# Image parts of V and K in pairs of column blocks in a fused cross-attention kernel

## Chip, cores and metric

One core of one Trainium2 chip. The metric is the device time of the program in microseconds (us), given as the median of several runs. The kernel before took 403.87 us (403.3 to 404.85 in 3 runs).

## The reference

Cross attention with 69 text tokens and 8 image tokens (4 dummies, 4 for boxes), 2 batches, 2048 queries, width 640, 20 heads of 32, context width 1024, all in fp32. Text and image tokens have their own projections and their own softmax:

```
q = split_heads(x @ w_q);  k = split_heads(text @ w_k);  v = split_heads(text @ w_v)
out_text = merge_heads(softmax(q k^T / sqrt(32)) v)
k_ip = split_heads(ip_h @ w_k_ip);  v_ip = split_heads(ip_h @ w_v_ip)
out_ip = merge_heads(softmax(q k_ip^T / sqrt(32) + mask_ip) v_ip)
out = (out_text + out_ip) @ w_out + b_out + x
```

The mask comes from which boxes hold a query's place on a 64x32 grid.

## The kernel before

The queries are cut into 8 tiles of 512 (2 batches, 4 tiles each), the width of 640 into 5 column blocks of 128 (4 heads). A unit `c` is one tile and one column block; there are 40. For every unit TensorE (PE) makes q (15 products of 128x512, each operand split in a high and a low part, L637), the scores (L668), O (L682) and the output product (again L637). The work is pipelined: in step `c` PE makes the scores of unit c+1 and q of unit c+2, then O of unit c-2 and, from step 6 on, the output of unit c-6. VectorE (DVE) subtracts the maximum, sums and transposes, ScalarE (ACT) takes the exponential and copies results out of PSUM, GpSimd (POOL) multiplies by the reciprocal sums and makes low parts. SP issues nearly all DMAs; ACT issues four per step. Each engine has one program, written out by hand, with waits on semaphores; the order in each is the order of the code.

K and V are made in the early steps, up to step 5, between the other work: one column block `g` of 128 at a time, five of each. For one block there are

- a text part (`text_part`, L714): eight matmuls, over the context width, 138 columns in a PSUM bank;
- an image part (`image_part`, L720): eight matmuls whose stationary operand is 32 columns of the context (16 image tokens of both batches, padded). Matmul kt writes to the 32 partitions 32*(kt % 4), so that four partial sums stand one below the other in a 128x128 range of a bank, from column 256 (`PART_COL`);
- a copy of this range by ACT to `img_part` (L409 for K, L414 for V);
- a fold (L738, L753): a matmul with a 0/1 matrix that adds the four partial sums into the image columns beside the text part;
- copies, and for V a transposition on PE (L758).

K of block g is made two steps ahead of V of the same block. The blocks of K are in banks 5 and 7, the text and image parts of V in bank 6. The weights come by DMA, 512 KB for each block and kind, into few places: two for K (`wk_raw`, `wki_raw`), three for V (`wv_raw`, `wvi_raw`). A load into a used place waits for a fold that shows the place free: K's block g waits until the fold of block g-2 is done (`kt_made`), V's blocks 3 and 4 for the folds of blocks 0 and 2 (`vt_made`). In SP's program the loads of K's block 4 come in step 0 behind three loads of x.

In steps 0 to 5 (`early_step`) PE has, in this order: the scores; O; the K fold of block c+2; V's text part for c < 3; V's image part of block c-1; four q products; V's fold; five q products; V's transposition; six q products; then for c < 2 K's text and image part of block c+3, otherwise V's text part of block c.

Of the kernel before, what the change touches and what calls it, by code (L numbers as in the profile page):

```python
# [8 lines left out]
ACT = mybir.ActivationFunctionType  # L9
AX_X = mybir.AxisListType.X  # L10

P = 128
# [3 lines left out]
TOKENS = 77  # L16
# [32 lines left out]
def xattn_kernel(nc, x, ctx, bbox, grid, eye, w_q, w_k, w_v, w_k_ip, w_v_ip, w_out, b_out, out):  # L49
# [1 line left out]

    at = {}
    LINE, ROW = 64, W * 4
    top = [-(-nc.sbuf_base // ROW) * ROW]

    def sb(name, shape, dt=F32):

# [13 lines left out]
        return es.enter_context(nc.semaphore(name))  # L71

    with es:
        x_hi = sb("x_hi", [P, BATCH, KD, W], F32R)
        x_lo = sb("x_lo", [P, BATCH, KD, W], F32R)
        o_hi = sb("o_hi", [P, BATCH, KD, W], F32R)
# [13 lines left out]
        eye_sb = sb("eye_sb", [P, P + BATCH * IMG])  # L90
        ident = eye_sb[:, 0:P]
        fold = eye_sb[:, P:P + BATCH * IMG].rearrange("p (b n) -> p b n", b=BATCH)
        vt = sb("vt", [P, BATCH, TOKENS])
        mask = sb("mask", [P, BATCH, TILES, QT, IMG])
        bias = sb("bias", [P, KD])
        box = sb("box", [P, BATCH, BOXES, 4])
# [3 lines left out]
        den = sb("den", [P, 2, 2, QT * HG])  # L100
        rden = sb("rden", [P, 2, 2, QT * HG])
        scratch = sb("scratch", [P, BATCH * TILES * QT * (2 * BOXES + 1) + 2 * BATCH * BOXES])
        img_part = sb("img_part", [P, 2, P])
        res = sb("res", [P, 2, W])


# [15 lines left out]

        WARM_BANK, WARM = 3, 11
        V_BANK, PART_COL = 6, 256
        K_BANKS = [5, 7, 5, 5, 5]
        K_PART_BANKS = [6, 7, 5, 5, 5]
        k_places = [ps[:, bank, 0:BATCH * TOKENS].rearrange("p (b n) -> p b n", b=BATCH) for bank in K_BANKS]
# [242 lines left out]
        @block.scalar  # L370
        def _(act):
            def high(job):

                what, n = job
                number = NUMBER[job]
                slot = stage[:, number % KD, :]
                act.wait_ge(stage_loaded[number % KD], 16 * (number // KD + 1))
                if what == "x":
                    b, _, kt = place(n)
                    if n >= 2 * KD:  # L380
                        act.wait_ge(q_made, (n // KD - 1) * KD)
                    nc.scalar.activation(x_hi[:, b, kt, :], slot[:, 0:W], ACT.Copy).then_inc(stage_hi, 1)  # L382
                else:
                    hi = {"w_q": wq_hi, "w_out": wo_hi}[what]
                    nc.scalar.activation(hi[:, n, :], slot, ACT.Copy).then_inc(stage_hi, 1)

            def copy_q(c):
                act.wait_ge(q_made, c + 1)
                if c >= 2:
                    act.wait_ge(scores_made, c - 1)  # L390
                nc.scalar.activation(q[:, c % 2, :], ps[:, Q_BANK, :], ACT.Copy, scale=SCALE).then_inc(q_copied, 1)  # L391

            def exp(c):
                act.wait_ge(shifted, c + 1)
                nc.scalar.activation(prob[:, c % 2, :, 0:TOKENS], prob[:, c % 2, :, 0:TOKENS], ACT.Exp).then_inc(exp_done, 1)  # L395

            def move_rest(c):

                act.wait_ge(turned, c + 1)
                if c >= 2:  # L400
                    act.wait_ge(o_made, c - 1)
                for a in range(QB):
                    act.dma_start(prob_k[2 * SQ:2 * SQ + SQ // 2, c % 2, a, :, :],  # L403
                                  prob_t[SQ * a:SQ * a + SQ // 2, c % 2, 2, :, :]).then_inc(moved[c % 2], 16)

            def copy_k_part(g):

                act.wait_ge(k_part_made, g + 1)
                nc.scalar.activation(img_part[:, 0, :], ps[:, K_PART_BANKS[g], PART_COL:PART_COL + P], ACT.Copy).then_inc(k_part_copied, 1)  # L409

            def copy_v_part(g):

                act.wait_ge(v_part_made, g + 1)
                nc.scalar.activation(img_part[:, 1, :], ps[:, V_BANK, PART_COL:PART_COL + P], ACT.Copy).then_inc(v_part_copied, 1)  # L414

            def copy_k(g):

                act.wait_ge(kt_made, g + 1)
                nc.scalar.activation(k[:, :, g, :], k_places[g], ACT.Copy).then_inc(k_copied, 1)

            def copy_vt(g):

                act.wait_ge(vt_made, g + 1)
                if g > 0:
                    act.wait_ge(v_made, g)
                nc.scalar.activation(vt[:, :, :], v_place, ACT.Copy).then_inc(vt_copied, 1)

            def copy_v(g):

                act.wait_ge(v_made, g + 1)  # L430
                nc.scalar.activation(v[0:TOKENS, :, P * g:P * g + P], v_turned, ACT.Copy).then_inc(v_copied, 1)

            def o_high(c):
                b, t, g = place(c)
                act.wait_ge(o_made, c + 1)
                if c >= 2 * KD:
                    act.wait_ge(out_made, (c // KD - 1) * KD)
                nc.scalar.activation(o_hi[:, b, g, :], ps[:, O_BANK, :], ACT.Copy).then_inc(o_hi_done, 1)  # L438

            def prologue():  # L440
                high(("w_q", 0))
                for kt in range(KD):
                    act.wait_ge(x0_loaded[kt], 16)
                    nc.scalar.activation(x_hi[:, 0, kt, :], x0_raw[:, kt, :], ACT.Copy).then_inc(x0_hi, 1)
                copy_q(0)
                copy_k_part(0)
                copy_k(0)
                high(("w_q", 1))
                high(("w_q", 2))
                copy_q(1)  # L450
                copy_k_part(1)
                exp(0)
                copy_k(1)
                copy_k_part(2)
                high(("w_q", 3))

            def step(c):
                if c <= KD:
                    if c + AHEAD_K < KD:
                        copy_k(c + AHEAD_K)  # L460
                    if c > 0:
                        copy_v_part(c - 1)
                    if c > 2:
                        o_high(c - 2)
                    if c > 0:
                        copy_vt(c - 1)
                        copy_v(c - 1)
                    exp(c + AHEAD_S)
                    copy_q(c + AHEAD_Q)
                    if c == 2:  # L470
                        o_high(c - 2)
                    if c + AHEAD_K + 1 < KD:
                        copy_k_part(c + AHEAD_K + 1)
                else:
                    o_high(c - 2)
                    if exists(c + AHEAD_S):
                        exp(c + AHEAD_S)
                    if exists(c + AHEAD_Q):
                        copy_q(c + AHEAD_Q)
                if c == 0:  # L480
                    high(("w_q", 4))
                move_rest(c)
                for job in step_jobs(c):
                    high(job)

            def epilogue():
                for c in range(UNITS - 2, UNITS):
                    o_high(c)

            turns(prologue, step, epilogue)  # L490
# [139 lines left out]
        def _(pe):  # L630
# [82 lines left out]
                    text = ctx_sb[:, kt, 0:BATCH * TEXT].rearrange("p (b n) -> p b n", b=BATCH)  # L713
                    nc.tensor.matmul(dst[:, :, 0:TEXT], raw[:, kt, :], text, start=(kt == 0), stop=(kt == KC - 1))  # L714

            def image_part(bank, raw, made):

                for kt in range(KC):
                    rows = slice(IMG_PAD * (kt % 4), IMG_PAD * (kt % 4) + IMG_PAD)
                    last = nc.tensor.matmul(ps[rows, bank, PART_COL:PART_COL + P], ctx_sb[:, kt, BATCH * TEXT:CTX_COLS],  # L720
                                            raw[:, kt, :], start=(kt < 4), stop=(kt >= 4))
                last.then_inc(made, 1)

# [5 lines left out]

            def k_image(g):  # L730
                pe.wait_ge(wki_loaded[g % K_SLOTS], 16 * (g // K_SLOTS + 1))
                image_part(K_PART_BANKS[g], wki_raw[:, g % K_SLOTS, :, :], k_part_made)

            def k_fold(g):
                if g == 0:
                    pe.wait_ge(eye_loaded, 16)
                pe.wait_ge(k_part_copied, g + 1)
                nc.tensor.matmul(k_places[g][:, :, TEXT:TOKENS], img_part[:, 0, :], fold,  # L738
                                 start=True, stop=True).then_inc(kt_made, 1)

            def v_text(g):
# [4 lines left out]

            def v_image(g):
                pe.wait_ge(wvi_loaded[V_SLOT[g]], 16 * (V_ROUND[g] + 1))
                image_part(V_BANK, wvi_raw[:, V_SLOT[g], :, :], v_part_made)

            def v_fold(g):
                pe.wait_ge(v_part_copied, g + 1)
                nc.tensor.matmul(v_place[:, :, TEXT:TOKENS], img_part[:, 1, :], fold, start=True, stop=True).then_inc(vt_made, 1)  # L753

            def v_turn(g):
                pe.wait_ge(vt_copied, g + 1)
# [22 lines left out]
            def early_step(c):  # L779
# [8 lines left out]
                else:  # L788
                    if c < 3:
                        v_text(c - 1)  # L790
                    v_image(c - 1)
                    make_q(c + AHEAD_Q, whole[0:4])
                    v_fold(c - 1)
                    make_q(c + AHEAD_Q, whole[4:9])
# [3 lines left out]
                    make_o(c - 2)  # L798
                if c < 2:
                    k_text(c + AHEAD_K + 1)  # L800
                    k_image(c + AHEAD_K + 1)
                elif c < KD:
                    v_text(c)

# [76 lines left out]
```

## Time and profile before

| | us |
|---|---|
| median of 3 runs | 403.87 |
| profiled execution, whole time | 404.16 |
| its span, first to last instruction | 402.3 |
| PE busy (share of the span) | 393.6 (98%) |
| DVE busy | 336.9 (84%) |
| POOL busy | 156.1 (39%) |
| ACT busy | 129.1 (32%) |
| DMA queue of SP, share of 16 engines | 54.6% |

The chain of work that ended last is PE's for 86%. The mean granted clock of PE is 0.997 of full speed. Matmul durations in the rows overlap each other, since matmuls are pipelined; what one costs is read from start to start. Each fp32 matmul of the image and text parts leaves two records (x16 for eight).

### The profile page before, as it was taken

Reading aid. Unit: us, or ns where it says so; the run is one execution under the profiler, and the core shown is the slowest. Engines: PE = TensorE matmul, PEld = TensorE weight load, DVE = VectorE, ACT = ScalarE, POOL = GpSimd, SP = SyncE. Lnnn points to the kernel's source line nnn. Section 1 sums busy time; section 2 is a strip of 40 time slices with the busy share of each in tenths; the row PEclk is TensorE's granted clock in tenths of the full one; section 3 lists DMA queues with packets and bytes.
Section 4 is the critical chain, followed back from the end, with each engine's and each line's share of the span. In section 5 each row is a group of like instructions: output and inputs, shape, how many; then the busy total and the mean of one; then the engine's idle time right before and its main releaser. Section 6 shows DMA issues by size and latency. Waiting matters only on the chain.

```text
span 402.3 us, 10795 instructions
## 1 busy us (share of the span) xinstructions
PE 393.6 (98%) x4452; PEld 292.3 (73%) x4452; DVE 336.9 (84%) x458; ACT 129.1 (32%) x196; POOL 156.1 (39%) x128
## 2 busy tenths in 40 slices
PE   8899999999999999999999999999999999999995
PEld 7688868577777776777777767777777677776773
DVE  4559779898899998998998999999989999999503
ACT  5236334453333322432323322343223322321100
POOL 0336622687326433364226442462227532222200
PEclk9999999999999999999999999999999999999998
DMA  8999736576657454764457454664466544544555
GB/s 280 382 374 333 206 78 233 158 232 171 182 158 223 132 139 138 196 190 138 137 168 231 124 148 135 209 172 145 121 211 193 142 131 127 156 124 119 178 158 182
DMA packets 42849, 72.96 MB, mean 181 GB/s; under 512 B 10544, under 2 KB 10672, under 8 KB 42800
## 3 DMA queue, kind: packets, MB, share of 16 engines
q1 hardware_dynamic: 37680, 67.02, 54.6%
q10 hardware_dynamic: 5120, 5.25, 5.2%
q8 instruction: 35, 0.57, 0.6%
q14 instruction: 14, 0.11, 0.1%
HBM read 35.53 MB, written 10.49 MB: 114 GB/s over the span
## 4 chain that ended last, share of the span: by engine, by line
PE 86%; DVE 3%; SPq 3%; DMA 3%; ACT 2%; issue 1%; ACTq 1%; DVEq 0%
PE ps L637 63%; PE ps L682 9%; PE ps L668 9%; PE ps L714 3%; SPq L259 2%; DMA wk_raw<-in_w_k 2%; ACT prob L395 1%; PE ps L720 1%; ACTq L403 1%; DVE text_max L501 1%; DVE prob L507 1%; ACT q L391 1%; DMA out_tiles<-res 1%; SPq L279 1%; DMA prob_k<-prob_t 1%
## 5 line engine op out<-in xcount | busy, mean ns | idle before, releaser
L357 POOL TENSOR_TENSOR prob<-prob,rden 128x1104 f32<-128x1104 f32 x40 | 82.2, 2056 | 200.5 <-DVE rden L530 200.5
L395 ACT ACTIVATE prob<-prob 128x1232 f32<-128x1232 f32 x40 | 50.0, 1250 | 65.7 <-DVE prob L518 65.7
L537 DVE STREAM_TRANSPOSE prob_t<-prob 128x1536 f32<-128x1536 f32 x40 | 70.7, 1767 | 0.2 <-POOL prob L359 0.2
L501 DVE TENSOR_REDUCE text_max<-ps 128x16 f32<-128x1104 f32 x40 | 52.1, 1303 | 17.1 <-PE ps L668 16.2
L637 PE MATMUL ps<-x_hi,wq_hi 128*128 128x512 f32 x200 | 59.2, 418 | 0.1
L637 PEld LDWEIGHTS ps<-x_hi,wq_hi 128*128 128x128 f32 x200 | 34.6, 188 | 33.9 <-issue 28.1
L525 DVE TENSOR_REDUCE den<-prob 128x16 f32<-128x1104 f32 x40 | 50.6, 1265 | 7.3 <-ACT prob L395 7.2
L438 ACT ACTIVATE o_hi<-ps 128x512 fp32r<-128x512 f32 x40 | 23.7, 592 | 101.9 <-PE ps L682 98.1
L637 PE MATMUL ps<-o_hi,wo_hi 128*128 128x512 f32 x200 | 55.6, 392 | 0.0
L637 PE MATMUL ps<-o_hi,wo_lo 128*128 128x512 f32 x200 | 55.1, 389 | 0.0
L637 PE MATMUL ps<-o_lo,wo_hi 128*128 128x512 f32 x200 | 55.1, 389 | 0.0
L637 PE MATMUL ps<-x_hi,wq_lo 128*128 128x512 f32 x200 | 54.4, 394 | 0.0
L637 PE MATMUL ps<-x_lo,wq_hi 128*128 128x512 f32 x200 | 52.6, 390 | 0.0
L507 DVE TENSOR_TENSOR prob<-ps,text_max 128x1104 f32<-128x1104 f32 x40 | 52.0, 1300 | 0.0
L341 POOL TENSOR_TENSOR x_lo<-stage,x_hi 128x512 fp32r<-128x512 f32 x35 | 45.1, 1314 | 2.7 <-ACT x_hi L382 2.6
L637 PEld LDWEIGHTS ps<-o_hi,wo_hi 128*128 128x128 f32 x200 | 37.4, 188 | 11.0 <-issue 3.4
L555 DVE SCALAR_TENSOR_TENSOR res<-ps,bias,res 128x512 f32<-128x512 f32 x37 | 27.3, 739 | 19.9 <-DMA res<-in_x 11.7
L682 PE MATMUL ps<-prob_k,v 77*32 77x512 f32 x320 | 43.3, 604 | 0.2
L637 PEld LDWEIGHTS ps<-x_lo,wq_hi 128*128 128x128 f32 x200 | 37.7, 189 | 7.8
L637 PEld LDWEIGHTS ps<-x_hi,wq_lo 128*128 128x128 f32 x200 | 37.6, 189 | 7.9 <-issue 0.2
L637 PEld LDWEIGHTS ps<-o_lo,wo_hi 128*128 128x128 f32 x200 | 37.5, 188 | 7.8
L637 PEld LDWEIGHTS ps<-o_hi,wo_lo 128*128 128x128 f32 x200 | 37.5, 188 | 7.8
(58 smaller groups left out, 346.4 us busy)
## 6 DMA issues: line engine op xcount, KB each, us to landing
prob_k<-prob_t SPq DMA_DIRECT2D x320, 64.0 KB
stage<-in_x SPq DMA_DIRECT2D x38, 256.0 KB, 3.0
res<-in_x SPq DMA_DIRECT2D x37, 256.0 KB
out_tiles<-res SPq DMA_DIRECT2D x37, 256.0 KB, 2.2
prob_k<-prob_t ACTq DMA_DIRECT2D x160, 32.0 KB
wki_raw<-in_w_k_ip SPq DMA_DIRECT2D x5, 512.0 KB, 7.0
wk_raw<-in_w_k SPq DMA_DIRECT2D x5, 512.0 KB, 6.7
wv_raw<-in_w_v SPq DMA_DIRECT2D x5, 512.0 KB, 8.9
```

The costliest lines, as they stand in the source:

```text
L341: nc.gpsimd.tensor_tensor(x_lo[:, b, kt, :], slot[:, 0:W], x_hi[:, b, kt, :].bitcast(F32), ALU.subtract).then_inc(stage_lo, 1)
L357: nc.gpsimd.tensor_tensor(e[:, :, 0:TEXT], e[:, :, 0:TEXT], rden[:, par, 0, :].unsqueeze(2).to_broadcast([P, QT * HG, TEXT]), ALU.mult)
L395: nc.scalar.activation(prob[:, c % 2, :, 0:TOKENS], prob[:, c % 2, :, 0:TOKENS], ACT.Exp).then_inc(exp_done, 1)
L438: nc.scalar.activation(o_hi[:, b, g, :], ps[:, O_BANK, :], ACT.Copy).then_inc(o_hi_done, 1)
L501: nc.vector.tensor_reduce(text_max[:, par, :, :], s[:, :, :, 0:TEXT], AX_X, ALU.max).then_inc(text_max_done, 1)
L507: nc.vector.tensor_tensor(e[:, :, :, 0:TEXT], s[:, :, :, 0:TEXT], text_max[:, par, :, :].unsqueeze(3).to_broadcast([P, QT, HG, TEXT]), ALU ...
L525: nc.vector.tensor_reduce(den[:, par, 0, :], e[:, :, 0:TEXT], AX_X, ALU.add)
L537: nc.vector.transpose(prob_t[:, c % 2, :, :, :].rearrange("p k n r -> p n k r"), prob[:, c % 2, :, :].rearrange("p n (k r) -> p n k r", r= ...
L555: nc.vector.scalar_tensor_tensor(out=tile, in0=ps[:, bank, :], scalar=bias[:, c % KD:c % KD + 1], in1=tile, op0=ALU.add, op1=ALU.add).then ...
L637: return nc.tensor.matmul(ps[:, bank, :], w[:, g, P * kt:P * kt + P], m[:, b, kt, :], start=(n == 0), stop=(n == 3 * KD - 1))
L668: last = nc.tensor.matmul(ps[at:at + P // 2, j, TOKENS * n:TOKENS * n + TOKENS], q[rows, c % 2, P * n + at:P * n + at + P // 2], k[rows, b ...
L682: last = nc.tensor.matmul(ps[DH * j:DH * j + DH, O_BANK, :], v[0:TOKENS, b, P * g + DH * j:P * g + DH * j + DH], p_k[:, :, :, j, :], start ...
```

## The change

It makes the image parts of V's blocks 0 and 1 together in step 1, of blocks 2 and 3 together in step 3, of block 4 alone in step 5; those of K's blocks 3 and 4 together in step 0. K's blocks 0, 1 and 2 stay as they were. The second block of a pair goes to columns 384 to 511 of the same bank. ACT copies both ranges with one instruction of 256 columns, after both are made; `img_part` has room for two per kind. The folds stay one by one, where they were. `img_part` grows by 1 KB per partition; `vt` moves to the front of the memory, before the rounding of x_hi's address to 2 KB. Nothing else is changed, no load either.

```diff
-    top = [-(-nc.sbuf_base // ROW) * ROW]
+    top = [-(-nc.sbuf_base // LINE) * LINE]
...
+        vt = sb("vt", [P, BATCH, TOKENS])
+        top[0] = -(-top[0] // ROW) * ROW
...
-        vt = sb("vt", [P, BATCH, TOKENS])
...
-        img_part = sb("img_part", [P, 2, P])
+        img_part = sb("img_part", [P, 2, 2, P])
...
+        V_PAIRS, K_PAIRS = {0: 2, 2: 2, 4: 1}, {0: 1, 1: 1, 2: 1, 3: 2}
+        V_PLACE, K_PLACE = (0, 1, 0, 1, 0), (0, 0, 0, 0, 1)
...
             def copy_k_part(g):
-                act.wait_ge(k_part_made, g + 1)
-                nc.scalar.activation(img_part[:, 0, :], ps[:, K_PART_BANKS[g], PART_COL:PART_COL + P], ACT.Copy).then_inc(k_part_copied, 1)
+                n = K_PAIRS[g]
+                act.wait_ge(k_part_made, g + n)
+                nc.scalar.activation(img_part[:, 0, 0:n, :], ps[:, K_PART_BANKS[g], PART_COL:PART_COL + n * P].rearrange("p (n d) -> p n d", d=P),
+                                     ACT.Copy).then_inc(k_part_copied, n)
...
-                    if c > 0:
+                    if c - 1 in V_PAIRS:
                         copy_v_part(c - 1)
...
-                    if c + AHEAD_K + 1 < KD:
+                    if c + AHEAD_K + 1 in K_PAIRS:
                         copy_k_part(c + AHEAD_K + 1)
...
-            def image_part(bank, raw, made):
+            def image_part(bank, col, raw, made):
...
-                    last = nc.tensor.matmul(ps[rows, bank, PART_COL:PART_COL + P], ctx_sb[:, kt, BATCH * TEXT:CTX_COLS],
+                    last = nc.tensor.matmul(ps[rows, bank, col:col + P], ctx_sb[:, kt, BATCH * TEXT:CTX_COLS],
...
-                image_part(K_PART_BANKS[g], wki_raw[:, g % K_SLOTS, :, :], k_part_made)
+                image_part(K_PART_BANKS[g], PART_COL + P * K_PLACE[g], wki_raw[:, g % K_SLOTS, :, :], k_part_made)
...
-                nc.tensor.matmul(k_places[g][:, :, TEXT:TOKENS], img_part[:, 0, :], fold,
+                nc.tensor.matmul(k_places[g][:, :, TEXT:TOKENS], img_part[:, 0, K_PLACE[g], :], fold,
...
-                    v_image(c - 1)
+                    for g in range(V_PAIRS.get(c - 1, 0)):
+                        v_image(c - 1 + g)
...
-                    k_image(c + AHEAD_K + 1)
+                    for g in range(K_PAIRS.get(c + AHEAD_K + 1, 0)):
+                        k_image(c + AHEAD_K + 1 + g)
```

`copy_v_part`, `v_image` and `v_fold` change as those of K do.

PE, from the last text part of step 0 (K, block 3) to the scores of step 1 before; `wki_loaded1` and `wki_loaded0` are the semaphores of the two places for K's image weights, block 3 is in the second, block 4 in the first.

```order
L714 MATMUL ps<-ctx_sb,wk_raw 128x2x69 [waits k_copied,wk_loaded1]
L714 MATMUL ps<-ctx_sb,wk_raw 128x2x69 x7
L720 MATMUL ps<-wki_raw,ctx_sb 32x128 [waits wki_loaded1]
L720 MATMUL ps<-wki_raw,ctx_sb 32x128 x7
L668 MATMUL ps<-k,q 64x77 [waits scores_used,k_copied,q_copied]
```

The same place in the changed kernel, up to the scores and the fold behind them.

```order
L721 MATMUL ps<-ctx_sb,wk_raw 128x2x69 [waits k_copied,wk_loaded1]
L721 MATMUL ps<-ctx_sb,wk_raw 128x2x69 x7
L727 MATMUL ps<-wki_raw,ctx_sb 32x128 [waits wki_loaded1]
L727 MATMUL ps<-wki_raw,ctx_sb 32x128 x7
L727 MATMUL ps<-wki_raw,ctx_sb 32x128 [waits wki_loaded0]
L727 MATMUL ps<-wki_raw,ctx_sb 32x128 x7
L675 MATMUL ps<-k,q 64x77 [waits scores_used,k_copied,q_copied]
L675 MATMUL ps<-k,q 64x77 x31
L745 MATMUL ps<-eye_sb,img_part 128x2x8 [waits k_part_copied]
```

The eight image matmuls of block 4 moved up by one step, with their wait for the load, ahead of the scores of step 1.

PE from the end of step 1 (K's text part of block 4) to the q products of step 2, before.

```order
L714 MATMUL ps<-ctx_sb,wk_raw 128x2x69 x7
L720 MATMUL ps<-wki_raw,ctx_sb 32x128 [waits wki_loaded0]
L720 MATMUL ps<-wki_raw,ctx_sb 32x128 x7
L668 MATMUL ps<-k,q 64x77 [waits scores_used,k_copied,q_copied]
L668 MATMUL ps<-k,q 64x77 x31
L738 MATMUL ps<-eye_sb,img_part 128x2x8 [waits k_part_copied]
L714 MATMUL ps<-ctx_sb,wv_raw 128x2x69 [waits v_copied,wv_loaded1]
L714 MATMUL ps<-ctx_sb,wv_raw 128x2x69 x7
L720 MATMUL ps<-wvi_raw,ctx_sb 32x128 [waits wvi_loaded1]
L720 MATMUL ps<-wvi_raw,ctx_sb 32x128 x7
L637 MATMUL ps<-x_hi,wq_hi 128x512 [waits stage_lo,q_copied]
```

The same place in the changed kernel.

```order
L721 MATMUL ps<-ctx_sb,wk_raw 128x2x69 x7
L675 MATMUL ps<-k,q 64x77 [waits scores_used,k_copied,q_copied]
L675 MATMUL ps<-k,q 64x77 x31
L745 MATMUL ps<-eye_sb,img_part 128x2x8 [waits k_part_copied]
L721 MATMUL ps<-ctx_sb,wv_raw 128x2x69 [waits v_copied,wv_loaded1]
L721 MATMUL ps<-ctx_sb,wv_raw 128x2x69 x7
L644 MATMUL ps<-x_hi,wq_hi 128x512 [waits stage_lo,q_copied]
```

Both groups of image matmuls are gone from here; V's went one step up, K's to the place shown before.

ACT from the copy of q in step 0 to the copy of V's first image part, in the changed kernel.

```order
L394 ACTIVATE q<-ps 128x512 [waits scores_made,q_made]
L413 ACTIVATE img_part<-ps 128x256 [waits k_part_made]
L388 ACTIVATE wq_hi<-stage 128x640 [waits stage_loaded4]
L406 DMA prob_k<-prob_t 16x512 [waits turned]
L406 DMA prob_k<-prob_t 16x512 x3
L385 ACTIVATE x_hi<-stage 128x512 [waits stage_loaded0]
L385 ACTIVATE x_hi<-stage 128x512 [waits stage_loaded1]
L385 ACTIVATE x_hi<-stage 128x512 [waits stage_loaded2]
L426 ACTIVATE k<-ps 128x2x77 [waits kt_made]
L420 ACTIVATE img_part<-ps 128x256 [waits v_part_made]
```

The order is that of before; the two copies into `img_part` had 128 columns, and the first of them now waits for both blocks of K.

## Rows read from the trace of the kernel before

**Rows 1.** Windows view, 26 to 32 us: busy time (instructions) by engine, clock, DMA, GB/s

```profile
26.00:32.00 6.00, 6.00 (x49) 5.07 (x48) 5.93 (x7) 1.85 (x3) 3.95 (x3) 1.00 0.97 356
```

**Rows 2.** Chain that ended last: start us, us, what; one steady step's products

```profile
80.49 7.04 PE ps L637 x30
```

**Rows 3.** Timeline of PE: start us, us, what [idle before <-releaser]; the two late gaps

```profile
74.60 0.40 PE L753 MATMUL ps<-eye_sb,img_part 128*128 128x16 f32 x2 [0.17 <-ACT img_part L414]
...
78.54 0.95 PE L668 MATMUL ps<-k,q 32*64 32x77 f32 x64 [0.71 <-ACT q L391]
```

**Rows 4.** Timeline of PE, end of step 0

```profile
29.55 2.04 PE L714 MATMUL ps<-ctx_sb,wk_raw 128*128 128x138 f32 x16
31.52 0.65 PE L720 MATMUL ps<-wki_raw,ctx_sb 128*32 128x128 f32 x16
32.23 0.95 PE L668 MATMUL ps<-k,q 32*64 32x77 f32 x64
```

**Rows 5.** Timeline of SP, the issues of K's block 4

```profile
26.87 0.45 SPq L246 DMA_DIRECT2D wk_raw<-in_w_k  x1
27.36 0.74 SPq L246 DMA_DIRECT2D wki_raw<-in_w_k_ip  x1
```

**Rows 6.** DMA view, 27.2 to 27.8 us: issue, count, size, us to landing

```profile
wki_raw<-in_w_k_ip SPq DMA_DIRECT2D x1, 512.0 KB, 7.8
```

**Rows 7.** Chain that ended last, first text weights of K

```profile
4.49 7.85 DMA wk_raw<-in_w_k
12.38 2.15 PE ps L714 x16
```

**Rows 8.** Timeline of PE, steps 1 to 6, what stands around the image parts

```profile
42.21 0.64 PE L720 MATMUL ps<-wki_raw,ctx_sb 128*32 128x128 f32 x16
42.78 0.95 PE L668 MATMUL ps<-k,q 32*64 32x77 f32 x64
...
43.91 2.13 PE L714 MATMUL ps<-ctx_sb,wv_raw 128*128 128x138 f32 x16
45.97 0.65 PE L720 MATMUL ps<-wvi_raw,ctx_sb 128*32 128x128 f32 x16
46.54 1.20 PE L637 MATMUL ps<-x_hi,wq_hi 128*128 128x512 f32 x4
...
60.67 2.04 PE L714 MATMUL ps<-ctx_sb,wv_raw 128*128 128x138 f32 x16
62.64 0.95 PE L668 MATMUL ps<-k,q 32*64 32x77 f32 x64
63.52 1.06 PE L682 MATMUL ps<-prob_k,v 77*32 77x512 f32 x8
64.40 0.62 PE L720 MATMUL ps<-wvi_raw,ctx_sb 128*32 128x128 f32 x16
64.95 1.20 PE L637 MATMUL ps<-x_hi,wq_hi 128*128 128x512 f32 x4
...
79.42 1.06 PE L682 MATMUL ps<-prob_k,v 77*32 77x512 f32 x8
80.42 1.42 PE L637 MATMUL ps<-x_hi,wq_hi 128*128 128x512 f32 x5
```

**Rows 9.** Timeline of ACT, the copy of K's image part of block 3

```profile
32.24 0.28 ACT L409 ACTIVATE img_part<-ps 128x128 f32<-128x128 f32 x1
```

**Rows 10.** Timeline of PE, start of the span

```profile
1.05 5.06 PE L764 MATMUL ps<-q 128*128 128x128 f32 x22 [1.05 <-DVE q L592]
...
6.65 0.63 PE L637 MATMUL ps<-x_hi,wq_lo 128*128 128x512 f32 x1
7.08 0.43 PE L637 MATMUL ps<-x_lo,wq_hi 128*128 128x512 f32 x1
```

**Rows 11.** Windows view, end of the span (columns as rows 1)

```profile
397.00:398.00 1.00, 0.47 (x3) 0.04 (x1) 1.00 (x2) 0.00 (x0) 0.00 (x0) 1.00 0.01 2
...
400.00:401.00 1.00, 0.00 (x0) 0.00 (x0) 0.00 (x0) 0.00 (x0) 0.00 (x0) 0.50 1.04 399
```

More of the change, by code:

```diff
@@ L406, in copy_k_part @@
             def copy_k_part(g):
-                act.wait_ge(k_part_made, g + 1)
-                nc.scalar.activation(img_part[:, 0, :], ps[:, K_PART_BANKS[g], PART_COL:PART_COL + P], ACT.Copy).then_inc(k_part_copied, 1)
+                n = K_PAIRS[g]
+                act.wait_ge(k_part_made, g + n)
+                nc.scalar.activation(img_part[:, 0, 0:n, :], ps[:, K_PART_BANKS[g], PART_COL:PART_COL + n * P].rearrange("p (n d) -> p n d", d=P),
+                                     ACT.Copy).then_inc(k_part_copied, n)
             def copy_v_part(g):
-                act.wait_ge(v_part_made, g + 1)
-                nc.scalar.activation(img_part[:, 1, :], ps[:, V_BANK, PART_COL:PART_COL + P], ACT.Copy).then_inc(v_part_copied, 1)
+                n = V_PAIRS[g]
+                act.wait_ge(v_part_made, g + n)
+                nc.scalar.activation(img_part[:, 1, 0:n, :], ps[:, V_BANK, PART_COL:PART_COL + n * P].rearrange("p (n d) -> p n d", d=P),
+                                     ACT.Copy).then_inc(v_part_copied, n)
             def copy_k(g):
@@ L748, in v_image @@
                 pe.wait_ge(wvi_loaded[V_SLOT[g]], 16 * (V_ROUND[g] + 1))
-                image_part(V_BANK, wvi_raw[:, V_SLOT[g], :, :], v_part_made)
+                image_part(V_BANK, PART_COL + P * V_PLACE[g], wvi_raw[:, V_SLOT[g], :, :], v_part_made)
             def v_fold(g):
                 pe.wait_ge(v_part_copied, g + 1)
-                nc.tensor.matmul(v_place[:, :, TEXT:TOKENS], img_part[:, 1, :], fold, start=True, stop=True).then_inc(vt_made, 1)
+                nc.tensor.matmul(v_place[:, :, TEXT:TOKENS], img_part[:, 1, V_PLACE[g], :], fold, start=True, stop=True).then_inc(vt_made, 1)
             def v_turn(g):
```

## The prediction

> **What bounds the kernel now.** I read the busy shares first. TensorE (PE) works 98% of the span, and the loads are heavy early: from 26 to 32 us PE is busy for all 6.00 us while the DMA engines are 97% taken at 356 GB/s [rows 1]. In the chain of work that ended last the steady part reads as one pattern repeated: scores, O, thirty 128x512 products in 7.04 us, 0.235 us each [rows 2]. In the timeline of PE hardly a gap is left: after the first 16 us there are two, 0.17 us at 74.6 and 0.71 us before the scores at 78.54 [rows 3]. The second is short of a reserve: it ends when ScalarE has copied q, and q's copy stands behind the exponential and the copy of V, which PE's own transposes released shortly before, so it moves along with PE. So the kernel is bound by PE's order, from the first step to the end. A microsecond in which PE must wait in the early steps is a microsecond at the end, and a microsecond of PE work taken out is one gained. VectorE and ScalarE have slack in these steps and follow PE.
>
> What has to be looked at is therefore (a) how long the image matmuls hold PE, alone and behind each other, and (b) whether their weights are there at the earlier places.
>
> **The K pair: the weights of block 4 are not there.** Before, PE begins step 0's last text part at 29.55, block 3's eight image matmuls at 31.52 and the scores at 32.23 [rows 4]. Block 4's image matmuls came a whole step later, at 42.21 [rows 8]. Now they stand between the image matmuls of block 3 and these scores. Their load is issued by SP at 27.36 [rows 5], since it waits for the third K fold and stands behind three loads of x and the text weights; the change moves no row of SP. Its time to landing was 7.8 us [rows 6]. These 7.8 us count from the start of the issue: the first text weights of K, issued at 4.49, land after 7.85 us, at 12.34, and PE begins on them at 12.38, 0.04 later [rows 7]. So block 4's image weights land at 27.36 + 7.8 = 35.16 and PE can start on them at 35.20. Eight such matmuls up to the start of the scores take 42.78 - 42.21 = 0.57 us [rows 8]. The scores start at 35.77 in place of 32.23: **+3.54 us**.
>
> What of this is hidden? Nothing on PE: the wait stands at the head of its queue, and behind it are the scores of unit 2, the K fold, V's text part and all the rest. On ScalarE the copy of the K parts, which ran at 32.24 [rows 9], now asks for both blocks and waits until about 35.8. Queued behind it are the rounding of the last block of w_q, four DMAs of step 0's probabilities, three roundings of x, a copy of K and the first copy of V parts. They slide by about 3.6 us, as PE's own places for them do (the q product that needs w_q's last block comes a step later), so I charge nothing more. VectorE gets its scores 3.5 us later; it was itself behind with unit 1 when they came, so it loses less than that and stays ahead of PE's demand. SP's load of V's block 3, whose guard is V's first fold, slips with PE; it is used two steps later.
>
> The landing itself could move. Down: the four DMAs of ScalarE, 32 KB each, no longer start at 32.24 but after the wait, and their 0.13 MB at 356 GB/s [rows 1] are 0.37 us of the engines. Up: nothing new is ahead of the load. So the delay lies between 3.17 and 3.54 us by this; I take 3.54, since the engines serve other queues as well and the share that falls to this load is not shown. On this the Trainium skill says, in Trainium Kernel Development and Optimization, Key Constraints, that DMAs issued from SP, ACT and POOL run on the same 16 engines and interleave. By that rule the load would land up to 0.37 us earlier and the time would be lower by as much; the trace of before doesn't show this load without those four.
>
> **What comes back at the later places.**
> - K, step 1: block 4's image matmuls are gone. Text part to scores with nothing between is 62.64 - 60.67 = 1.97 us [rows 8]; text part to image matmuls is also 31.52 - 29.55 = 1.97 [rows 4]. What goes is 42.78 - 42.21 = 0.57: **-0.57**. (Their work at the new place is inside the 3.54.)
> - V, step 2: block 1's go. Before: 45.97 - 43.91 = 2.06 and 46.54 - 45.97 = 0.57 [rows 8], together 2.63 from the text part to the q products; without them I take 1.97, the longer of what a text part costs here: -0.66.
> - V, step 4: block 3's go. Before, O to image is 64.40 - 63.52 = 0.88 and image to q 64.95 - 64.40 = 0.55; O to q directly is 80.42 - 79.42 = 1.00 [rows 8]: -0.43.
> - Added at steps 1 and 3: a second eight directly behind the first. A row of sixteen isn't in the trace. From below, eight matmuls that need no change of the array's form cost 0.88 + 0.55 - 1.00 = 0.43, the net figure just seen; from above 0.57, the price when alone. I take 0.43, because both boundaries of a pair are already paid for by the first eight: +0.86.
> - Sum for V: -0.66 - 0.43 + 0.86 = **-0.23** (from above +0.05).
> - ScalarE loses three copies and has three of 256 columns for 128, hidden: in V's places four q products of over 1 us stand between the image matmuls and the fold.
> - vt moves ahead of x_hi in memory: an address, no instruction; nothing.
>
> Without any effect on the clock: 3.54 - 0.57 - 0.23 = **+2.74 us**.
>
> **The clock.** The stall makes PE idle from about 32.15 (31.52, 0.43 and the last matmul's tail) to 35.20, some 3.05 us, longer than any gap of before. What does that do? At the end of the span PE's last matmul ends at about 397.5 and the granted clock is 0.50 over all of 400 to 401 [rows 11]: it fell from 2.4 to 1.2 GHz at most 2.5 us after PE went idle. So a pause of 3.05 us is long enough for it to fall. The price from below is 0 (it doesn't fall, or rises as soon as PE works). From above: at the start PE works from 1.05 on, and products still start 0.43 us apart at 6.65 and 7.08 [rows 10], against 0.235 later [rows 2]; some 6.0 us at half pace give away (1 - 0.235/0.43) x 6.0 = 2.7 us. The pause is a single one in a busy stretch, nearer to neither end; I take the middle, **+1.4 us**. The Trainium skill, TensorE: Matmul & The Clock Gate, The HAM clock gate, says likewise that the array runs at 1.2 GHz after it was idle and gets back to 2.4 GHz after sustained activity. By that rule the fall is to be expected and the sum stays as it is; that a single pause in the middle of the work does it, no row of this kernel shows.
>
> **Sum.** 404.16 (the profiled execution's own time; its span is 402.3, with 1.9 around it) + 2.74 + 1.4 = 408.3. The profiled execution is 0.29 over the median of the runs shown (403.87). Against that median: **408.0 us**, 1% slower.
>
> **Rivals.**
> 1. *The pause costs only itself.* The clock stays at 2.4 GHz, as it did through the 0.71 us gap of rows 3. For it: the pause is short, and the fall at the end came with nothing at all behind it. Against: the 2.5 us of rows 11. Time: 403.87 + 2.74 = 406.6. With the load 0.37 us earlier 406.2.
> 2. *The clock stays low for as long as at the start.* 403.87 + 2.74 + 2.7 = 409.3, and a little more if the pair's second eight cost 0.57 each (409.6).
> 3. *Not slower: the transfer is there.* The mechanism: block 4's image weights land before PE comes to them, because the load, issued at 27.36, gets a larger share of the engines in this program. The place is the end of step 0 and the price is that of the whole stall: without it K gives 0.43 - 0.57 = -0.14, V -0.23, and the time is 403.5. It decides from a landing 3.2 us earlier on (by 31.95, in 4.6 us rather than 7.8); with one only 0.72 us earlier and no loss by the clock the result comes within 0.5% of before. Against it: the row before shows all engines at 97% in this stretch, the same loads stand ahead of it in the same order, and nothing is removed from them before 32.2.
> 4. *The lost time is caught up later.* The early steps hold waits of PE of 0.88 us in all, and those come from ScalarE's place behind PE. If both vanished, 405.7 with no clock effect. I give it little.
>
> **Chances.** Forecast (stall with a fall of the clock that costs 0.7 to 2.2): 0.50, 407.3 to 408.9. Rival 1: 0.27. Rival 2: 0.13. Rival 3: 0.04. Rival 4: 0.06. A measurement of this kernel tells about 0.5% (2.0 us) from no change. Slower than that, above 405.9: all of the forecast, of rival 2 and nearly all of rival 1, 0.89. Within: part of 1, 3 and 4, 0.10. Faster, under 401.9, has no mechanism beyond 0.37 us: 0.01. The range: 406.0 (rival 1 with an early landing) to 409.9 (rival 2 with a dearer pair) leaves out rivals 3 and 4 and some at the top.
>
> **What would show it.** In the profile after: PE's row of sixteen image matmuls of K broken by a wait of about 3.1 us for the DMA into wki_raw, the scores behind it at about 35.8 (anything before 33 and the main term is wrong); the waits table with that DMA as PE's largest single one; the granted clock at half for a stretch between 34 and 41 us, with products 0.43 us apart (at 1.00 throughout, rival 1); text to scores in step 1 at 1.97 with nothing between; V's pairs 1.0 us long rather than 1.14; the steady step still 8.9 to 9.0 us. The prediction is wrong if the load's landing isn't at 35, if the lag of 2.74 at 43 us isn't the lag at 300 us, or if steps 1 to 5 run shorter than PE's rows say.

## The result and the profile after

The changed kernel took 409.34 us in the median (407.76 to 410.76, 6 runs), the kernel before 403.94 us (402.83 to 404.85, 6 runs). The ratio is 1.0133 (95% interval 1.0102 to 1.0164). Forecast were 408.0 us and a range of 406.0 to 409.9. The profiled execution took 409.87 us, its span is 408.1 (before 404.16 and 402.3), so it is one of the longer ones.

The page gives the granted clock of PE in tenths of full speed, for 40 equal slices of the span, here of 10.2 us each. In the kernel before only the last slice is under 9; after, the fourth (30.6 to 40.8 us) is at 7.

```profile
span 408.1 us, 10795 instructions
...
PEclk9997999999999999999999999999999999999999
```

The timeline of PE, in the stretch of [rows 4] and on through [rows 8] (start us, us, what, idle before and what ended it):

```profile
30.82 2.15 PE L721 MATMUL ps<-ctx_sb,wk_raw 128*128 128x138 f32 x16 [0.95 <-DMA wk_raw<-in_w_k]
32.90 0.65 PE L727 MATMUL ps<-wki_raw,ctx_sb 128*32 128x128 f32 x16
36.38 1.08 PE L727 MATMUL ps<-wki_raw,ctx_sb 128*32 128x128 f32 x16 [2.83 <-DMA wki_raw<-in_w_k_ip]
37.38 1.42 PE L675 MATMUL ps<-k,q 32*64 32x77 f32 x64
...
39.18 3.90 PE L721 MATMUL ps<-ctx_sb,wv_raw 128*128 128x138 f32 x16
43.01 1.08 PE L727 MATMUL ps<-wvi_raw,ctx_sb 128*32 128x128 f32 x32
44.02 1.21 PE L644 MATMUL ps<-x_hi,wq_hi 128*128 128x512 f32 x4
...
48.02 2.04 PE L721 MATMUL ps<-ctx_sb,wk_raw 128*128 128x138 f32 x16
49.99 0.95 PE L675 MATMUL ps<-k,q 32*64 32x77 f32 x64
...
51.12 2.13 PE L721 MATMUL ps<-ctx_sb,wv_raw 128*128 128x138 f32 x16
52.99 1.17 PE L644 MATMUL ps<-x_hi,wq_hi 128*128 128x512 f32 x4
```

The scores, at 32.23 in [rows 4], start at 37.38. Between the two image groups of K stands the wait for `wki_raw`, and what follows is slow: V's text part takes 43.01 - 39.18 = 3.83 us, where it took 2.06 in [rows 8]. From 44.02 on the durations are the old ones. The windows view of the same stretch (us, then busy time and instructions of PE, PEld, DVE, ACT, POOL, then the granted clock, DMA share and GB/s) says why:

```profile
34.00:35.00 1.00, 0.00 (x0) 0.00 (x0) 0.04 (x1) 0.00 (x0) 0.88 (x1) 1.00 1.00 401
35.00:36.00 1.00, 0.00 (x0) 0.00 (x0) 0.00 (x0) 0.00 (x0) 1.00 (x1) 0.99 1.05 410
36.00:38.00 2.00, 1.62 (x53) 1.21 (x56) 0.00 (x0) 0.42 (x2) 0.55 (x2) 0.50 1.07 299
...
42.00:43.00 1.00, 1.00 (x6) 0.87 (x4) 1.00 (x2) 0.06 (x1) 1.00 (x2) 0.60 0.57 154
43.00:44.00 1.00, 1.00 (x33) 0.81 (x32) 1.00 (x1) 0.00 (x0) 1.00 (x2) 1.00 0.23 72
```

The clock fell just before 36, in the wait, and rose in the last quarter of 42 to 43: some 6.8 us at 0.50, that is at 1.2 GHz, nearly all of it under work. The load itself, in the timeline of SP and in the DMA view of the issues at 28.4 to 28.6 us, as [rows 5] and [rows 6]:

```profile
28.46 0.89 SPq L249 DMA_DIRECT2D wki_raw<-in_w_k_ip  x1
```

```profile
wki_raw<-in_w_k_ip SPq DMA_DIRECT2D x1, 512.0 KB, 7.9
```

It was issued 1.1 us later than in the profile of before and took as long, 28.46 + 7.9 = 36.4. The change touches no load; the text weights of block 3 were late too (the 0.95 us in the first row above). In the profiles of the kernels below whose loads are in the same order this issue stands anywhere from 27.43 to 29.03 us, and the load lands 6.3 to 8.0 us behind it, so this is how much one execution differs from another. A late issue need not be a late landing: with the latest, at 29.03, PE began on the weights at 35.33.

Most of the lag stays. The same scores, before and after:

```profile
301.77 0.95 PE L668 MATMUL ps<-k,q 32*64 32x77 f32 x64
```

```profile
307.54 0.95 PE L675 MATMUL ps<-k,q 32*64 32x77 f32 x64
```

They are 5.77 us apart, and the two profiled times differ by 409.87 - 404.16 = 5.71.

### The profile page after: what moved, and what is told of

Read it like the earlier page. It is cut to its first block, busy times and chain, and to the rows that moved or that the text cites. A ratio compares the mean times of both kernels' runs of the same rounds, so it can differ in the third digit from the quotient of the medians.

```text
span 408.1 us, 10795 instructions
## 1 busy us (share of the span) xinstructions
PE 394.8 (97%) x4452; PEld 294.4 (72%) x4452; DVE 337.4 (83%) x458; ACT 128.9 (32%) x193; POOL 155.7 (38%) x128
## 4 chain that ended last, share of the span: by engine, by line
PE 82%; DMA 7%; SPq 5%; DVE 3%; issue 1%; ACT 1%; ACTq 1%; DVEq 0%
PE ps L644 59%; PE ps L675 9%; PE ps L689 8%; PE ps L721 4%; SPq L262 2%; DMA out_tiles<-res 2%; DMA wk_raw<-in_w_k 2%; DMA wki_raw<-in_w_k_ip 2%; PE ps L727 1%; DVE prob_t L544 1%; DMA res<-in_x 1%; ACTq L406 1%; DVE text_max L508 1%; DVE prob L514 1%; SPq L249 1%
## 5 line engine op out<-in xcount | busy, mean ns | idle before, releaser
L562 DVE SCALAR_TENSOR_TENSOR res<-ps,bias,res 128x512 f32<-128x512 f32 x37 | 27.2, 736 | 19.5 <-DMA res<-in_x 11.4
```

Source lines behind the costliest of these rows:

```text
L562: nc.vector.scalar_tensor_tensor(out=tile, in0=ps[:, bank, :], scalar=bias[:, c % KD:c % KD + 1], in1=tile, op0=ALU.add, op1=ALU.add).then ...
```

## The experiments

Theory A was the prediction's: all of the loss arises at K's pair, from PE's wait for block 4's image weights and from the clock that falls in it. Against it stood: pairs cost by themselves (B), V's block 1 comes too early (C), the clock is of no matter, ScalarE's queue behind its longer wait has a share. Ratios are to the kernel before in the same comparison, with 95% intervals.

### The pairs of V alone

```diff
-        V_PAIRS, K_PAIRS = {0: 2, 2: 2, 4: 1}, {0: 1, 1: 1, 2: 1, 3: 2}
-        V_PLACE, K_PLACE = (0, 1, 0, 1, 0), (0, 0, 0, 0, 1)
+        V_PAIRS, K_PAIRS = {0: 2, 2: 2, 4: 1}, {g: 1 for g in range(KD)}
+        V_PLACE, K_PLACE = (0, 1, 0, 1, 0), (0, 0, 0, 0, 0)
```

> The pairs of V alone; the image parts of K one by one at their old places. Theory A (the time is lost at K's pair: the wait for the image weights of block 4 and the clock that falls behind it): no wait for wki_raw and no fall of the clock before the end of the span; 403.7 us, between 403.2 and 404.2 (V's rows give 0.23 us less than before). Theory B (sixteen image matmuls in a row, or one copy for two blocks, cost by themselves): two of the three pairs are still there, so most of the loss stays, 407 us or more. Theory C (a part of the loss is V's block 1 made before its place): 1 to 2 us over before.

Measured: 403.47 us, ratio 0.999 (0.9965 to 1.0014). B and C fall. PE's timeline:

```profile
35.89 1.08 PE L727 MATMUL ps<-wvi_raw,ctx_sb 128*32 128x128 f32 x32
36.90 1.20 PE L644 MATMUL ps<-x_hi,wq_hi 128*128 128x512 f32 x4
...
44.59 2.13 PE L721 MATMUL ps<-ctx_sb,wv_raw 128*128 128x138 f32 x16
46.46 1.18 PE L644 MATMUL ps<-x_hi,wq_hi 128*128 128x512 f32 x4
```

A pair takes 36.90 - 35.89 = 1.01 us, against 0.57 for one block: the second eight cost 0.44, the estimate's 0.43. With nothing between, V's text part to q takes 1.87 us, where 1.97 was taken. V's two pairs therefore save 0.3 us, which is too little for this measurement to show.

### The pair of K alone

```diff
-        V_PAIRS, K_PAIRS = {0: 2, 2: 2, 4: 1}, {0: 1, 1: 1, 2: 1, 3: 2}
-        V_PLACE, K_PLACE = (0, 1, 0, 1, 0), (0, 0, 0, 0, 1)
+        V_PAIRS, K_PAIRS = {g: 1 for g in range(KD)}, {0: 1, 1: 1, 2: 1, 3: 2}
+        V_PLACE, K_PLACE = (0, 0, 0, 0, 0), (0, 0, 0, 0, 1)
```

> The pair of K alone; V's image parts one by one. Theory A: PE waits about 3 us for wki_raw before block 4's image matmuls, the granted clock falls to half for a stretch behind it, and all of the loss is there and 0.2 us more: 409.5 us, between 407 and 411. Theory B: one pair of three, about a third of the loss, 405.7 us.

Measured: 409.17 us, ratio 1.0133 (1.0104 to 1.0161), the ratio of the whole change. PE's timeline:

```profile
31.83 0.65 PE L727 MATMUL ps<-wki_raw,ctx_sb 128*32 128x128 f32 x16
35.33 1.08 PE L727 MATMUL ps<-wki_raw,ctx_sb 128*32 128x128 f32 x16 [2.85 <-DMA wki_raw<-in_w_k_ip]
...
42.49 1.19 PE L644 MATMUL ps<-x_hi,wq_hi 128*128 128x512 f32 x4
```

From the end of the wait to the q products of step 1 it takes 42.49 - 35.33 = 7.16 us. At the full clock this is 0.57 for the eight [rows 8] and 35.98 - 32.23 = 3.75 from the scores [rows 4] to these products in the kernel before, 4.32 together. The clock costs the difference, 2.84 us. The products in the kernel before, and the text part that follows them:

```profile
35.98 1.20 PE L637 MATMUL ps<-x_hi,wq_hi 128*128 128x512 f32 x4
...
40.24 2.04 PE L714 MATMUL ps<-ctx_sb,wk_raw 128*128 128x138 f32 x16
```

### The wait filled with useless work

```diff
                     for g in range(K_PAIRS.get(c + AHEAD_K + 1, 0)):
+                        if g == 1:
+                            for _ in range(12):
+                                nc.tensor.matmul(ps[:, V_BANK, :], wq_hi[:, 0, 0:P], x_hi[:, 0, 0, :], start=True, stop=True)
                         k_image(c + AHEAD_K + 1 + g)
```

> The whole change with twelve extra products of 128x512 into the idle bank 6 between the image matmuls of block 3 and those of block 4 (some 2.8 us of work that is of no use; nobody reads it). The wait for the load becomes short, its end stays where it was. Theory A with the clock's share: the scores of step 1 start as late as in the changed kernel, but the clock stays at full speed, and the time is 406.6 us (405.8 to 407.3), about 2 to 3 under the changed kernel. Rival (the clock doesn't matter, or the loss is all the wait): the same time as the changed kernel, 409.3 us. If the work is added behind the wait rather than inside it, 412 us.

Measured: 406.22 us, ratio 1.0059 (1.0023 to 1.0095). More work on PE, and the kernel is some 3 us faster than the changed one. PE's timeline:

```profile
32.66 3.02 PE L812 MATMUL ps<-x_hi,wq_hi 128*128 128x512 f32 x12
35.94 0.64 PE L727 MATMUL ps<-wki_raw,ctx_sb 128*32 128x128 f32 x16 [0.26 <-DMA wki_raw<-in_w_k_ip]
36.51 0.95 PE L675 MATMUL ps<-k,q 32*64 32x77 f32 x64
...
40.70 1.19 PE L644 MATMUL ps<-x_hi,wq_hi 128*128 128x512 f32 x4
```

The load arrives no earlier than in the run of K's pair alone (35.94 and 35.33). But the eight image matmuls take 0.57 and the q products start 40.70 - 35.94 = 4.76 us after them, which is 0.57 + 3.75 and the 0.44 of V's second eight: nothing is slow. Its windows have the granted clock at 1.00 from 32 to 44 us. This separates the two parts of the loss: the wait alone, with the small savings of the pairs in it, is worth 406.22 - 404.17 = 2.05 us, the clock the remaining 3 or so. The filling doesn't hold the clock up for certain: one of the six runs took 408.31 us, with a mean granted clock of 0.994 where the other five have 0.999 or 1.000. It has no trace, so where its clock fell is not known.

### The kernel before with the wait alone, bare and filled

```diff
             def early_step(c):
+                if c == 1:
+                    pe.wait_ge(wki_loaded[0], 48)
                 make_scores(c + AHEAD_S)
```

> The kernel before with one thing more: PE waits, ahead of the scores of step 1, until the image weights of K's block 4 have landed. No image matmul is moved, no pair is made, ScalarE waits for nothing new. Theory A: this wait and the clock behind it are the whole loss of the pair of K; PE stands still for about 3 us, the clock falls to half, and the time is 409 us (407 to 410.5). Rival (what is queued on ScalarE behind the copy for both blocks has a share in the loss): clearly less, 406 to 407.

Measured: 408.19 us, ratio 1.011 (1.0062 to 1.0158). This kernel has no pair, and ScalarE waits for nothing new, and it has most of the loss. Its four runs are far apart, 406.34 to 410.73. PE's timeline:

```profile
35.06 1.25 PE L668 MATMUL ps<-k,q 32*64 32x77 f32 x64 [2.98 <-DMA wki_raw<-in_w_k_ip]
...
40.37 1.20 PE L637 MATMUL ps<-x_hi,wq_hi 128*128 128x512 f32 x4
```

Here 5.31 us pass from the scores to the q products instead of 3.75: 1.56 for the clock, about half of what the pair of K paid. The windows view shows it back at full speed from just before 39 us on, after some 3.4 us:

```profile
35.00:36.00 1.00, 0.94 (x64) 0.94 (x64) 0.00 (x0) 1.00 (x3) 1.00 (x2) 0.72 0.99 385
36.00:38.00 2.00, 2.00 (x26) 1.84 (x14) 1.66 (x3) 0.86 (x3) 2.00 (x3) 0.50 1.08 321
38.00:39.00 1.00, 1.00 (x7) 1.00 (x7) 1.00 (x1) 0.00 (x0) 1.00 (x2) 0.58 1.02 262
39.00:40.00 1.00, 1.00 (x16) 0.86 (x18) 0.93 (x3) 0.00 (x0) 1.00 (x2) 1.00 1.13 215
```

With the twelve products of the run above placed before this wait as well:

```diff
                 if c == 1:
+                    for _ in range(12):
+                        nc.tensor.matmul(ps[:, V_BANK, :], wq_hi[:, 0, 0:P], x_hi[:, 0, 0, :], start=True, stop=True)
                     pe.wait_ge(wki_loaded[0], 48)
```

> As the kernel before with the wait alone, and twelve useless products of 128x512 in front of it, into the idle bank 6. Theory A: PE is busy through the time of the wait, the clock stays, and what is left is the late start of the scores: 406.5 us (405.7 to 407.3), 2 to 3 under the kernel with the bare wait. Rival (the clock is no matter): both alike.

Measured: 406.18 us, ratio 1.006 (1.0039 to 1.0082), the same as the changed kernel filled. The two kernels with the wait bare and the two with it filled agree within their intervals, although one of each has the pairs and the other hasn't. So ScalarE's queue has no share that these runs can show.

The four runs of the bare wait also show that the clock need not fall. A stretch of 3.4 us at half speed takes 3.4 x 0.5 / 405 = 0.004 off the mean of an execution. The quickest run, 406.34 us, has a mean of 0.998, too high for such a stretch, and the time of the filled kernels; the slowest, 410.73 us, has 0.991.

### The load at another time

If the late load is the cause, an earlier load must cure it with all pairs in place. First with a place of its own, in `o_hi`, issued before the loads of x:

```diff
+        wki4_raw = over("wki4_raw", "o_hi", [P, KC, P])
...
                 load_k(3, wki_raw, w_k_ip, wki_loaded)
+                sp.dma_start(wki4_raw[:, :, :], w_k_ip[KD - 1]).then_inc(wki4_loaded, 16)
...
-                    load_k(4, wki_raw, w_k_ip, wki_loaded)
...
             def k_image(g):
+                if g == KD - 1:
+                    pe.wait_ge(wki4_loaded, 16)
+                    image_part(K_PART_BANKS[g], PART_COL + P * K_PLACE[g], wki4_raw[:, :, :], k_part_made)
+                    return
```

> The whole change, but K's image weights of block 4 get a place of their own (in o_hi, which is empty until step 2) and their load is issued in the prologue, before the three loads of x, with no wait for a fold. Theory A: they are issued near 25.4 and land near 32.5, so PE waits 0 to 1 us, the clock stays at full speed, and the time is 403.5 to 404.7 us, most likely 404.0. Theory B: pairs as before, so 408 to 410 us.

Measured: 403.44 us, just under the expected range, ratio 0.9984 (0.9967 to 1.0). The timelines of SP and of PE:

```profile
25.15 0.44 SPq L305 DMA_DIRECT2D wki_raw<-in_w_k_ip  x1
```

```profile
31.37 0.65 PE L729 MATMUL ps<-wki_raw,ctx_sb 128*32 128x128 f32 x16
32.47 0.65 PE L729 MATMUL ps<-wki_raw,ctx_sb 128*32 128x128 f32 x16 [0.46 <-DMA wki_raw<-in_w_k_ip]
33.04 0.95 PE L677 MATMUL ps<-k,q 32*64 32x77 f32 x64
```

A wait of 0.46 us remains. To remove it, the load goes still further up, behind V's block 1 in the prologue:

```diff
                 load_v(1, wvi_raw, w_v_ip, wvi_loaded)
+                sp.dma_start(wki4_raw[:, :, :], w_k_ip[KD - 1]).then_inc(wki4_loaded, 16)
```

> The whole change with a place of its own for K's image weights of block 4, as in the run before, but their load is issued still earlier, behind V's block 1, near 18.6 us. Theory A: they have long landed at 32 and PE waits for nothing there; the wait of 0.46 us of the run before is gone: 403.0 us, if the other loads are not later for it. Against it: the 512 KB ahead of the text weights of block 3 make these land about 1.3 us later, and PE waits for them before step 0's last text part: 404.3 us.

Measured: 405.1 us, 0.8 over the expectation's dearer side, ratio 1.0019 (0.9996 to 1.0041). In the profile the wait is gone, and another stands in its place, for the text weights one part earlier.

```profile
31.18 2.15 PE L723 MATMUL ps<-ctx_sb,wk_raw 128*128 128x138 f32 x16 [0.88 <-DMA wk_raw<-in_w_k]
33.25 1.08 PE L729 MATMUL ps<-wki_raw,ctx_sb 128*32 128x128 f32 x32
34.26 0.95 PE L677 MATMUL ps<-k,q 32*64 32x77 f32 x64
```

That is what the second side of the expectation named. One profile doesn't show it to be the cause, since the changed kernel, with these weights' load at its old position, waited 0.95 us for them too.

Last, the old places and the old guard, and only the order of SP's loads in step 0 changed:

```diff
+                if c == 0:
+                    load_k(4, wki_raw, w_k_ip, wki_loaded)
                 for job in step_jobs(c):
                     load(job)
                 if c == 0:
                     load_k(4, wk_raw, w_k, wk_loaded)
-                    load_k(4, wki_raw, w_k_ip, wki_loaded)
```

> The whole change, the old places, but SP issues the image weights of block 4 first in step 0, ahead of the three loads of x and of the text weights of block 4. Theory A: the load goes out when the third K fold is done, at 26.2 to 26.5 instead of 27.4 to 28.5, and has 1.25 MB less ahead of it; it lands at 32.5 to 34, PE waits 0.5 to 2 us, the clock stays in most runs: 404.5 us (403.5 to 405.5). Rival (the guard on the place, not the order of the loads, makes it late): 407 or more.

Measured: 403.41 us, just under the expected range, ratio 0.9988 (0.997 to 1.0006). The wait is 0.48 us:

```profile
31.55 0.64 PE L728 MATMUL ps<-wki_raw,ctx_sb 128*32 128x128 f32 x16
32.68 0.65 PE L728 MATMUL ps<-wki_raw,ctx_sb 128*32 128x128 f32 x16 [0.48 <-DMA wki_raw<-in_w_k_ip]
33.25 0.95 PE L676 MATMUL ps<-k,q 32*64 32x77 f32 x64
```

So the guard on the place is not what made it late; its position behind three loads of x and one of text weights is. None of these loads was needed soon: behind the 0.48 us PE waits for no DMA up to 90 us.

### Is a version better than both?

The two good versions once more, with 12 runs each and 23 of the kernel before.

> The kernel with the loads reordered once more, in more rounds, to see whether it is under the kernel before and not only level with it. From PE's rows: its pairs save 0.23 (V) and 0.14 (K), its wait for the load costs 0.5, so 0.1 us either way: a ratio to before of 0.9985 to 1.001. A gain by over 0.2% would mean that something else than the image parts is better in it.

> The kernel with a place of its own for block 4 once more, in more rounds. The same sum, with a wait of 0.46 us: a ratio to before of 0.9985 to 1.001.

Measured: reordered 403.34 us, ratio 0.9979 (0.9963 to 0.9994); own place 403.48 us, ratio 0.9982 (0.9965 to 0.9999). Both are just under the expected range, and under the kernel before by some 0.2%, 0.7 us, with intervals that just exclude no change. The sum from PE's rows gave 0.1; with the 1.87 us measured for V's text part it is V 0.31 + K 0.13 - the wait. That wait varies: it was 0.46 and 0.48 us in the profiles above, 0.37 in the new one of the reordered kernel and none in that of the own place, so the sum is 0 to 0.4 us. Whether the rest comes from the pairs or from the other order of the loads is open: the kernel before with its loads alone reordered was not tried.

## Why the prediction was right

The time lies in the range and the mechanism is the one forecast, at its place. The number is not the forecast's: 409.34 lies above its 407.3 to 408.9 and where rival 2 stood (409.3, chance 0.13). That it still lies in the range is in part luck, since errors cancel in the sum below. Step by step, for the profiled execution:

- *The bound.* A delay of PE in step 1 is one at the end: the lag is 6.0 us at 80 us, 5.77 at 300 and 5.71 in the profiled times.
- *The landing and the start of the scores.* Forecast: PE on block 4 at 35.20, scores at 35.77. Measured: 36.38 and 37.38; in K's pair alone 35.33. The time to landing was right in this profile (7.9 for 7.8) and is not a constant (6.3 in K's pair alone, issued at 29.03), the time of issue was that of one execution, and the eight matmuls ran at half clock (1.00 for 0.57). The possible gain of 0.37 us by ScalarE's postponed DMAs did not show: the load took 7.9, 6.3 and 8.0 us where they came behind it (changed kernel, K's pair, filled) and 7.8 and 7.6 where they were issued from 32.2 us on (kernel before, bare wait). The Trainium skill (Trainium Kernel Development and Optimization, Key Constraints) has the DMAs of SP, ACT and POOL interleave on the same 16 engines; no run here shows what that is worth.
- *What comes back.* K: text part to scores 49.99 - 48.02 = 1.97, as forecast. V: the second eight 0.44 for 0.43; the text part in front of q 1.87 for 1.97, 0.1 us too dear. V in all: -0.31 for -0.23.
- *The wait without the clock.* +2.74 was forecast for it; the filled kernel has 2.05 (0.9 to 3.8 by the interval of its ratio). The forecast is within it. The wait filled in the kernel before has 406.18 - 403.94 = 2.24. One thing that it could not see: in the profile of before the first O, in step 2, took 1.71 us, in every other profile here 1.06 or 1.07, so about 0.64 us of the path of that one execution are not paid elsewhere. What made it slow there stays open. The row of before:

```profile
50.62 1.71 PE L682 MATMUL ps<-prob_k,v 77*32 77x512 f32 x8
```

- *The clock.* This is the term that was mis-sized: "I take the middle, +1.4 us", between 0 and 2.7. Measured are 2.84 in K's pair alone and 1.56 in the kernel with the bare wait; for the changed kernel, from 36.38 to the q products at 44.02 are 7.64 us, where 0.57 + 3.75 + 0.44 = 4.76 are due at the full clock, so 2.88. It came out at the upper bound, rival 2's 2.7, in the profiled executions of both kernels with the pair, and near the middle in the one without. The mean granted clock of the six runs of the changed kernel was 0.990 to 0.994, against 0.996 or more in all but one run of the kernel before, so it fell in each of them, and by different lengths. Both grounds of this step were weaker than it took them to be. The 2.7 us rest on products 0.43 us apart at the start of the span; the windows view of before has the granted clock at 1.00 from 0 to 10 us, so half speed is read from the spacing alone, and that 2.7 is nearly 2.88 may be chance. The row of before for the place of these products:

```profile
6.00:7.00 1.00, 1.00 (x3) 0.83 (x3) 0.12 (x1) 0.77 (x2) 0.00 (x0) 1.00 0.99 367
```

And that 3.05 us are "long enough for it to fall" rests on the end of one span. After the last matmul of the changed kernel the clock still stood at 1.00 for over 4 us:

```profile
403.47 0.39 PE L644 MATMUL ps<-o_lo,wo_hi 128*128 128x512 f32 x1
```

```profile
407.00:408.00 1.00, 0.00 (x0) 0.00 (x0) 0.00 (x0) 0.00 (x0) 0.00 (x0) 1.00 0.04 12
```

So a pause of 3 us can bring the fall and need not; rival 1's chance was a real one.

- *The sum.* Forecast +4.1 on the median of before, measured +5.4 (409.34 - 403.94): the clock's 2.88 for 1.4 is about the difference, but other errors cancel beside it. From the profile of before to that of after the lag of PE is 4.15 us at block 4's image matmuls (36.38 - 32.23), and 8.04 at the q products of step 1 (44.02 - 35.98); in between come 0.57 and 0.44 for the second eights of K and V and the clock's 2.88. Then 0.57 of K go, as forecast, and 0.76 of V in step 2, for 0.66. So do the 0.64 us of the slow O, and 0.26 between the first q products of step 1 and K's text part (40.24 - 35.98 = 4.26 before, 48.02 - 44.02 = 4.00 after). V's second pair adds 0.43 and step 4 gives it back, which leaves 5.81. Against the forecast the landing is 1.2 us and the clock 1.5 us too long, and 0.9 us came back that no step of it had. The landing varies: in K's pair alone PE began at 35.33.

Rival 1 (the clock stays) is what the filled kernels show, at 406.2 instead of 406.6, but not the changed kernel. Rival 3 (the transfer is there) is what the load experiments made: 403.4, where it said 403.5. Rival 4 (caught up later) is wrong in its mechanism: the two waits of [rows 3] are still there, with 0.24 and 0.69 us. But the lag does shrink at other places, by the 0.26 and 0.64 us above, in steps 1 and 2.

## What to carry to other kernels

An operation that is pulled forward takes its wait for data along: before an edit that saves tenths on the engine, compare the landing of each load with the new place, and where it is late look for loads ahead of it in its queue that can wait. Here one load moved ahead of four others was worth 6 us, and the pairs some tenths at most. And a pause of about 3 us on TensorE cost up to twice its length here, because the work behind it ran at half clock; where it could not be removed, work that does nothing was better than none.

## What the runs showed of the hardware

- One pause of TensorE of 2.8 to 3.0 us in an otherwise full stretch brought the granted clock from 2.4 to 1.2 GHz, in all three profiled executions that had one. By the mean granted clock it did so in the six runs of the changed kernel, but not in one of the four with the bare wait (0.998, 406.34 us). Pauses of up to 1.21 us did not, in any profile.
- The length of a pause alone does not decide it. After the last matmul of a span the clock fell 2.2 us later in the kernel before, 2.5 to 3.9 in seven others and 4.2 in the changed kernel; in the other three (own place, both filled ones) it had not fallen when the span ended, 3.6 to 4.3 us after that matmul.
- The low stretch that follows differs in length: some 6.8 us in two of the three (cost 2.84 and 2.88 us of PE time), some 3.4 us in the third (1.56 us), although PE was busy behind the pause in all. In the two the clock fell 0.4 to 0.5 us before PE went on, in the third 0.4 us after. Whether this decides the length was not tried and stays open.
- Useless products of 128x512 in the pause, 3.02 us of them, kept the clock at 1.00 in both profiles and made the program 2 to 3 us shorter; one of the thirteen runs so filled has a mean of 0.994.
